# Graph attention layers on Trainium2: the skip projection moved into the aggregation, and ring buffers released at their exact last slot

## The reference

```python
for l in range(L):                      # L = 2
    q = (x @ Wq[l] + bq[l]).reshape(N, H, D)
    k = (x @ Wk[l] + bk[l]).reshape(N, H, D)
    v = (x @ Wv[l] + bv[l]).reshape(N, H, D)
    a = (q[dst] * k[src]).sum(-1) * scale
    amax = jax.ops.segment_max(a, dst, num_segments=N)
    e = jnp.exp(a - amax[dst])
    denom = jax.ops.segment_sum(e, dst, num_segments=N)
    alpha = e / (denom[dst] + 1e-16)
    agg = segment_sum(alpha[:, :, None] * v[src], dst).reshape(N, C)
    x = agg + (x @ Ws[l] + bs[l]) + enc
```

## Time and profile before

| what | value |
|---|---|
| median of 3 runs | 3170.1 us (3169.5 to 3174.96) |
| the profiled execution | 3169.63 us, span 3167.8 us |
| granted TensorE clock, mean | 0.908 |
| busy: PE, DVE, ACT, POOL | 2532.1, 2165.3, 1170.4, 1646.0 us |
| projection, layer 0 / 1 | 88 to 305 us / 1176 to 1368 us |
| scores, layer 0 / 1 | 309 to 750 us / 1371 to 1818 us |
| aggregation, layer 0 / 1 | 794 to 1160 us / 1861 to 2226 us |

### The profile page before, as it was taken

The page is one execution under the profiler, slowest core; times in us unless marked ns, Lnnn a source line. Parts: engine busy times, 40 slices in busy tenths (PEclk is TensorE's granted clock), DMA queues, the critical chain, the costliest instruction groups (busy, mean ns, idle before and its releaser), DMA issues. The chain is left out here.

```text
span 3167.8 us, 46485 instructions
## 1 busy us (share of the span) xinstructions
PE 2532.1 (80%) x9912; PEld 1863.5 (59%) x9912; DVE 2165.3 (68%) x3472; ACT 1170.4 (37%) x4350; POOL 1646.0 (52%) x1559
## 2 busy tenths in 40 slices
PE   1888777774988879977878669788785999599998
PEld 1766444442865557754545358556564767477776
DVE  5775778788966766657878888676474454566665
ACT  0554566664000021136666600000353322155554
POOL 0111767777677731146776777777132443255555
PEclk8999888887999989988888779999897999899999
DMA  2666777876677776667777757777432332251110
GB/s 101 243 233 239 238 234 246 248 231 193 190 215 223 216 235 217 198 215 240 241 242 239 226 153 214 218 222 221 157 133 93 115 111 93 102 163 41 40 45 34
DMA packets 244223, 574.89 MB, mean 181 GB/s; under 512 B 32642, under 2 KB 70894, under 8 KB 242834
## 3 DMA queue, kind: packets, MB, share of 16 engines
q0 software_dynamic: 100160, 328.28, 35.2%
q1 hardware_dynamic: 126546, 212.27, 19.7%
q10 hardware_dynamic: 17280, 31.63, 2.7%
HBM read 465.00 MB, written 107.06 MB: 181 GB/s over the span
## 5 line engine op out<-in xcount | busy, mean ns | idle before, releaser
L1319 POOL DMA_INDIRECT edge_ring<-v_rows,edges_src x626 | 616.0, 984 | 238.9 <-issue 128.2
L1319 POOL DMA_INDIRECT edge_ring<-k_rows,edges_src x626 | 591.8, 945 | 276.3 <-issue 128.2
L1628 PE MATMUL edge_psA<-layer_q_space 128*128 128x256 f32 (+1 forms) x2656 | 634.2, 392 | 107.7 <-DVE layer_q_space L1452 100.0
L1628 PEld LDWEIGHTS edge_psA<-layer_q_space 128*128 128x128 f32 x2656 | 493.2, 191 | 248.5 <-issue 180.9
L1452 DVE TENSOR_TENSOR layer_q_space<-edge_ring,edge_psQ 128x512 f32<-128x512 f32 x664 | 429.5, 683 | 175.4 <-SPq L1260 145.7
L1375 DVE TENSOR_TENSOR edge_ring<-edge_psQ,edge_ring 128x512 f32<-128x512 f32 x532 | 346.9, 683 | 131.9 <-ACT edge_ring L1464 64.4
L1464 ACT ACTIVATE edge_ring<-edge_ring 128x64 f32<-128x64 f32 x1328 | 320.0, 242 | 312.7 <-DVE edge_ring L1375 312.7
L1581 PE MATMUL edge_psQ<-layer_q_space,edge_hotT 128*128 x1064 | 363.8, 476 | 62.2 <-ACT edge_hotT L1489 36.1
L108 PE MATMUL proj_psP<-proj_w,proj_xT 128*128 128x512 f32 x1440 | 355.5, 404 | 12.5 <-DVE proj_xT L859 4.0
L1581 PEld LDWEIGHTS edge_psQ<-layer_q_space,edge_hotT 128*128 128x128 f32 x1064 | 237.7, 231 | 156.5 <-issue 103.9
L108 PEld LDWEIGHTS proj_psP<-proj_w,proj_xT 128*128 128x128 f32 x1440 | 271.6, 192 | 79.7 <-issue 9.1
(11 more groups left out here) (303 smaller groups left out, 3605.2 us busy)
## 6 DMA issues: line engine op xcount, KB each, us to landing
v_xT<-proj_xT SPq DMA_DIRECT2D x40, 512.0 KB, 4.8
edge_x_halves<-v_xT SPq DMA_DIRECT2D x80, 256.0 KB, 4.8
agg_rows<-layer_q_space ACTq DMA_DIRECT2D x40, 260.0 KB, 3.9
base_rows<-proj_enc SPq DMA_DIRECT2D x40, 256.0 KB, 2.1
k_rows<-proj_out ACTq DMA_DIRECT2D x40, 256.0 KB, 3.9
v_rows<-edge_ring ACTq DMA_DIRECT2D x40, 256.0 KB, 4.0
edge_ring<-k_rows,edges_src POOLq DMA_INDIRECT x626, 3.8
edge_ring<-v_rows,edges_src POOLq DMA_INDIRECT x626, 3.7
```

What stands on the lines that cost most here:

```text
L1319: pool.indirect_dma_start(ring[:, buffer[n], :], None, rows, bass.IndirectOffsetOnAxis(ap=T["src"][:, t:t + 1], axis=0)).then_inc(landed[b ...
L1628: last = pe.matmul(psA[:, bass.ds(d % 2, 1), e, 0:hi - lo].rearrange("p o w -> p (o w)"), hot[:, s % R, :], wv[:, s % R, lo:hi], start=Fal ...
```

## The change

1. **Skip in the aggregation.** The projections make K and Q alone; base in memory is at first bias + enc (x + bias in layer 0). S's weights go to memory beside V's (`skip_w`), both after tile 4. During the aggregation TensorE makes the 12 products of a node tile, three at the head of a batch (`project_skip`, batches 2 to 81), from halves of xT that SyncE loads again; VectorE adds them to base (`add_skip`), which SyncE loads and stores.
2. **Exact release.** The index makes `slots_of`, the last slot of each edge tile. SyncE reads it (`last_slots`), waits for that slot and counts `k_released` or `v_released` up; GpSimd waits for that count. SyncE releases AHEAD = 6 tiles before the gather's own.
3. **Banks.** V is projected into two banks in turn, spread rows have one, and `spread_row(j + 1)` stands behind the wait for batch j's one-hot tiles. K and Q use four banks in turn.
4. **Order.** Weight casts of the third and fourth matrix fall into tiles 0 to 3; V's first loads come after the third arrival; the V steps begin one batch later.

```diff
@@ projections, both layers @@
-        psP = [m.ps(f"psP{i}", [P, C]) for i in range(3)]
+        psP = [m.ps(f"psP{i}", [P, C]) for i in range(4)]
-                    if i == 1:
+                    if i == KC:
                         sp.wait_ge(w_lows, 4 * KC)
...
-                    sp.wait_ge(ready, i * 3 + S_ + 1)
+                    sp.wait_ge(biased, i + 1)
                     sp.dma_start(base_dram[i * P:(i + 1) * P, :], enc[:, i % 2, :]).then_inc(base_out[i % 2], 16)
...
-                    for j in range(3):
-                        if i:
-                            pe.wait_ge(ready, i * 3 + j - 2)
-                        else:
+                    for j in range(2):
+                        if i >= 2:
+                            pe.wait_ge(ready, i * 2 + j - 3)
+                        if i == 0:
                             pe.wait_ge(w_lows, (j + 1) * KC)
...
-                        if j == S_:
-                            vec.wait_ge(biased, i + 1)
-                            vec.tensor_tensor(enc[:, b, :], psP[j][:], enc[:, b, :], ALU.add).then_inc(ready, 1)
-                            continue
@@ edge_attention, SyncE @@
+                def release(r, used):
+                    if r < 0:
+                        return
+                    if r // B not in ends_of:
+                        ends_of.clear()
+                        ends_of[r // B] = last_slots(nc, sp, T, r // B * B, B)
+                    sp.wait_ge(used, ends_of[r // B][r % B])
+                    sp.sem_inc(k_released if used is multiplied else v_released, 1)
...
+                            release(t + AHEAD - NB, multiplied)
                             arrive(t, k_arrived)
...
+                for r in range(ET + AHEAD - NB, ET - 3):
+                    release(r, multiplied)
                 sp.wait_ge(queried, USED)
                 sp.dma_start(masks, T["mask_rows"]).then_inc(masks_in, 16)
+                sp.dma_start(skip_rows[:, 1:, :], later_v["skip_w"].rearrange("p (n c) -> p n c", c=C)
+                             ).then_inc(skip_in, 16)
...
+                for h in range(XH, 2 * NT):
+                    i, half = divmod(h - XH, 2)
+                    beside_block.setdefault((S_AT[i] + 1 + 2 * half) * B + 3 * B, []).append((load_half, 2 * NT + h))
+                for i in range(NT):
+                    beside_block.setdefault((S_AT[i] + 9) * B, []).append((store_base, i))
+                    if i + 2 < NT:
+                        beside_block.setdefault((S_AT[i] + 11) * B, []).append((load_base, i + 2))
                 sp.sem_inc(v_arrived, V_FIRST - 1)
                 for t in range(ET):
+                    if t + AHEAD < ET:
+                        release(t + AHEAD - NV, weighted)
                     arrive(ET + t, v_arrived)
+                    for do, i in beside_block.pop(t, ()):
+                        do(i)
@@ edge_attention, GpSimd @@
-                        pool.wait_ge(multiplied, t - NB + NT + 1)
+                        pool.wait_ge(k_released, t - NB + 1)
...
-                        pool.wait_ge(weighted, t - NV + NT + 1)
+                        pool.wait_ge(v_released, t - NV + 1)
@@ edge_attention, TensorE @@
+        S_AT = [2 + 4 * i for i in range(NT)]
+        s_steps = {S_AT[i] + k: (i, k) for i in range(NT) for k in range(KC)}
...
                 for s in range(USED):
+                    if s % B == 0 and s // B in s_steps:
+                        project_skip(*s_steps[s // B])
```

More of the change, by code:

```diff
@@ L894, in _, with w_low @@
                 normalise(1)
-                for i in range(4 * KC):
+                def w_low(i):
                     vec.wait_ge(w_highs, i + 1)
@@ L898, in _ @@
                                       ALU.subtract).then_inc(w_lows, 1)
+                for i in range(2 * KC):
+                    w_low(i)
                     if i == KC - 1:
@@ L922, in add @@
                     into = qsum[:] if j == Q_ else out[:, b, :]
[L923 removed]
+                    vec.tensor_tensor(into, psP[(2 * i + j) % 4][:], bias[:, j, :], ALU.add).then_inc(ready, 1)
                 for i in range(NT):
@@ L1311, in _ @@
+                for t in sorted(beside_block):
+                    for do, i in beside_block[t]:
+                        do(i)
+                for b in range(2):
+                    sp.wait_ge(base_out[b], 16 * (NT // 2))
             @block.gpsimd
@@ L1455, in _ @@
                                       ALU.mult).then_inc(weighted, 1)
+                for i in range(NT):
+                    if (S_AT[i] + 7) * B + 1 >= USED:
+                        add_skip(i)
             @block.scalar
@@ L1562, in project_v @@
                         pe.wait_ge(half_in[h % XH], h // XH * 16 + 16)
-                    product(pe, psV, [x_halves[:, h % XH, part, k % 2, :] for part in range(2)],
+                    product(pe, psV[i % 2], [x_halves[:, h % XH, part, k % 2, :] for part in range(2)],
                             [spare_row(part * KC + k) for part in range(2)], start=False, stop=(k == KC - 1)
@@ L1615, in _, with skip_row, project_skip @@
                     last.then_inc(returned, 1)
+                firsts = nc.alloc_registers(f"skip_parts_at{layer}", engines=[pe.engine])
+                nc.regs_mov(firsts, 1)
+                first = nc.snap(firsts, min_val=0, max_val=1)
+                def skip_row(n):
+                    return one(skip_rows[:, bass.ds(first + n, 1), :].bitcast(F32R))
+                def project_skip(i, k):
+                    if i == 0 and k == 0:
+                        pe.wait_ge(skip_in, 16)
+                    if i >= 2 and k == 0:
+                        pe.wait_ge(s_added, i - 1)
+                    h = 2 * NT + 2 * i + k // 2
+                    if k % 2 == 0:
+                        pe.wait_ge(half_in[h % XH], h // XH * 16 + 16)
+                    product(pe, psS[i % 2], [x_halves[:, h % XH, part, k % 2, :] for part in range(2)],
+                            [skip_row(part * KC + k) for part in range(2)], start=(k == 0), stop=(k == KC - 1)
+                            ).then_inc(s_projected, 1)
                 for s in range(USED):
+                    if s % B == 0 and s // B in s_steps:
+                        project_skip(*s_steps[s // B])
                     if s % B == 0:
```

193 lines of the change are left out of this document (126 added, 67 removed).

## The result

The changed kernel takes 3211.8 us, median of 4 runs (3207.5 to 3218.8), against 3170.2 us before: 1.0125 times the time, 95% interval 1.0103 to 1.0147. It is slower by about 42 us. I had forecast 3164, with a range that ended at 3205. The profiled execution has a span of 3217.1 us, 49.3 more than before; it is the slowest of the four, 7 us above their median.

A forecast was written before the change was run, and what follows sets the result against it. Layer 1's projection was bound by its load loop beside TensorE, layer 0's by the weight-unit loop, scores and aggregation by gathers. Terms -45 - 12 - 12 + 62 + 1 = -6 gave 3164 us by the median; range 3112 to 3205.

The forecast's parts named there:

- Projection, layer 1: S's work and the wait for x go, so a tile takes 6.50 us instead of 9.20; -45 us.
- Projection, layer 0: Fewer products gain only in the last tiles, earlier GpSimd sums and fewer early casts; -12 us.
- The unit loop: Layer 0's projection: ternary weight units run an 11.19 us loop without a matmul, so fewer products gain nothing there.
- The tail: Layer 0's projection, last two tiles without units: 12 products and one sum leave the path; 4 us gained.
- The collision with GpSimd: Layer 0's projection: GpSimd's sum covers VectorE's choosing; free to run earlier, it gains 0.4 us a tile, 7 in all.
- Rival E: Layer 0's projection: idle gaps lower TensorE's clock to 1.2 GHz, 56 us more, 3220; chance 0.03.
- Scores: Exact release removes most gather waits for VectorE, -15, and mask loads behind the last release cost +3; -12 in two layers.
- Aggregation, ring: Releases stand behind SyncE's loads that wait for products, so gather 48 goes 15.5 us later a layer; +31 us.
- Aggregation, pace: Halves and base add traffic, so each of 264 gathers a layer takes 0.012 us more; +6 us.
- rival D: Gathers: with four in flight, landings from 5.2 us on set the pace; at 5.6, 53 us more, 3217; chance 0.07.
- Aggregation, tail: The last half loads late, so last gather to end takes 21.8 us a layer against 9.4; +25 us.
- Rival A: The skip hides in the aggregation's idle TensorE time, taking the 62 us away, 3102; chance 0.10.

The follow-up runs named there:

- weights_apart: The changed kernel with S's weights stored in two parts, after tiles 14 and 16, instead of right behind V's after tile 4; 3196.1 us, 1.0101 of before.
- exact_alone: The kernel before with nothing but exact release added (table, SyncE's releases, GpSimd's new waits); 3141.8 us, 0.9945 of before.
- filled_clock: The changed kernel with 12 products a tile, whose bank nobody reads, put back in layer 0's projection; 3206.6 us, 1.0143 of before.
- skip_left_out: The changed kernel without the skip's products, sums, loads and stores in the aggregation; 3099.5 us, 0.9812 of before.
- slot_more_in_flight: loads_by_slot with six gathers in flight instead of four and release 12 tiles ahead instead of 6; 3041.6 us, 0.9631 of before.
- mixed_more_in_flight: mixed with six gathers in flight instead of four and release 12 tiles ahead instead of 6; 3037.8 us, 0.9624 of before.
- mixed: The changed kernel with layer 0's skip kept in its projection, layer 1's skip loads placed by slot, and the scores' old banks; 3126.1 us, 0.9899 of before.
- loads_by_slot: The changed kernel with the skip's loads and stores at tile 41 + 0.82 x slot instead of tile = slot + 8; 3153.3 us, 0.9989 of before.
- changed_six_only: The changed kernel with six gathers in flight instead of four and nothing else; 3120.7 us, 0.9850 of before.

## Why the prediction was wrong

The sum said -6 by the profiled execution, and +49 came (+42 by the medians). The steps that failed are the pace of the aggregation, where the limit of four in flight had been left out of the term, and the scores, where one edit had no price. Term by term:

- **Projection, layer 1: right, in part by luck.** -45 forecast, -48.4 measured. I took 6.50 us a tile and TensorE's 6.1 as next; it is TensorE, at 6.02. Against that the second store of weights took 5.5 us of its step (12.8, and 7.3 in weights_apart) where the sum has 2, and the mean step came out at 6.63.
- **Projection, layer 0: the mechanism right, two terms wrong.** The unit loop goes on: from tile 5 to tile 17 the Q sums take 135.6 us where they took 136.1. The tail gained 5, as said. The collision with GpSimd did shrink: VectorE's 132 choosing instructions took 38.3 us in all instead of 44.2. But the 7 us that I took from it did not come, since those steps gained only 0.5; this time is not on the loop's path. The second store of weights I had charged to layer 1 alone; the step where it falls grew by 7.5 here, some 5 of that its own. Rival E's premise came true, 0.84 of the clock, but its price did not: the idle time absorbs all of it. The Trainium skill, "TensorE: Matmul & The Clock Gate", "HAM oscillation", has the clock fall where TensorE waits between short bursts; the row's 0.84, and 0.95 with the bursts filled, agree.
- **Scores: wrong, a step that failed.** "Exact release should take most of this, and I count -15" holds by itself (-4.6 and -8.3 in exact_alone). What the prediction left out is the last edit, V's steps one batch later: it had stood in the list of changes, and no step priced it. It costs 17 us in two layers by one pair of executions, 7 to 21 by all of them, so about what exact release gives. I had put my doubt on the banks, which cost nothing that can be seen. The profiled execution adds to the miss: filled_clock, weights_apart and skip_left_out have the same scores and took 834 to 838 us for both layers, this execution 844.
- **Aggregation, ring: right in place and cause.** I had gather 48 at 825, 15.5 us late (15.2 by its own numbers), behind batch 7. It came 18.6 and 18.7 us later in the two layers, counted from the first v gather, and the rows show batch 7: its products end 31.7 us after the stage's first, where I had 31.2. The 3 us from there to the gather, in which SyncE issues the half and reads `slots_of`, I had at nothing.
- **Aggregation, pace: the step that failed most clearly.** I took "0.012 us more for each of 264", 6 us; it was 0.041 and 0.046, 23 us. I drew it from the scores' pace, which seemed to be the pace with halves beside it. Yet the cause was in rival D's hands: four in flight. I had set its threshold by the median, 3.7 us against 5.2. The median rose only to 4.4, under that threshold, and the gathers slowed all the same: from 900 to 1100 us the trace has 16 waits for landings, up to 1.6 us each, and with six in flight none is left. So the late landings count, not the median.
- **Aggregation, tail: right.** +25 forecast; 23.4 and 21.1 instead of 9.4 and 7.9, so +27.

The aggregation's ring, pace and tail come to 37 + 23 + 27 = 87, the whole of the third row. Of the 55 us between forecast and result, 23 are the scores (6 to 10 of them this execution's), 22 the aggregation (17 of them the pace), 11 layer 0; layer 1 gave 3 back and the rest took 3.

Rival A, that the skip hides, came nearly true in slot_more_in_flight: 424.8 / 421.5 us, the time without the skip at four in flight. It needed three other edits: the order, six in flight and release 12 ahead. And with the last two the stage without the skip takes 411.9 (layer 0 of mixed_more_in_flight), so 13 us a layer still do not hide.

For a DMA that GpSimd issues, the Trainium skill, "DMA: Bandwidth & Descriptors", "Anatomy of one DMA — SWDGE (gpsimd) path", fits about 2.0 us and the bytes over 436 GB/s; by that a gather of 256 KB would land in an estimated 2.6 us. From 900 to 1100 us the median is 3.7 in the kernel before and 4.4 in the changed one, so the rows decide.

## What to carry to other kernels

A queue that both waits for results and passes on permissions should have nothing in it that waits for a later result than the next permission; place such loads by the time when the consumer gets there, not by a number that only later runs in step. A limit on transfers in flight was set here by the late landings, not by the median: if gathers are slower than their interval of issue, try more in flight first, since it is an edit of one number. List every edit of a change with a price, the smallest too; here the unpriced one cost the scores some 7 to 21 us, about what exact release gave them. And take a stretch from more than one execution before a few us of it are put down to an edit.

## What the runs showed of the hardware

- Six indirect gathers of 256 KB in flight instead of four took 46 us from the kernel before (3111.1 against 3157.0) and 88 from mixed (3126.1 to 3037.8, with release 12 ahead, which alone did nothing). In mixed_more_in_flight a gather then goes every 1.250 us on the mean in the scores and the aggregation of both layers, once the ring is full. The landing itself does not get shorter (from 900 to 1100 us the median is 5.0 us in slot_more_in_flight, 4.6 in loads_by_slot).
- The DMA share reached 0.89 at 291 GB/s in slot_more_in_flight (900 to 1080 us of the span), and the gathers kept their interval (1.251 us on the mean of that layer).
- A wait that the trace puts on one releaser can vanish when another limit is lifted: from the changed kernel to changed_six_only 17.2 us for SyncE became 11.3, all of it in gaps of 0.3.
